# Attention on one core: score and value-sum matmuls alternate by pair of heads instead of by unit of four heads

## What is computed

```python
proj = quant4(x) @ ternary_weight(Wqkv_w).T + Wqkv_b      # q, k and v are views of it
q, k = (rotary(q, N), rotary(k, N))
ql, kl = (q @ U, k @ U)
att = jnp.einsum('bhnr,bhmr->bhnm', ql, kl) / math.sqrt(dk)
y = jax.nn.softmax(att, axis=-1) @ v
...
x = _layernorm(x + attention(x), axis=-1)
x = _layernorm(x + ffn(x), axis=-1)      # gated feed-forward, hidden width 1024, four layers
```

## Time and profile before

| | |
|---|---|
| Median of 3 runs | 2857.3 us (2856.99 to 2858.01) |
| Profiled execution: its own time | 2857.96 us |
| Profiled execution: span in the trace | 2856.3 us |
| Setup, until the first scores | 0 to 262 us |
| Attention | 262 to 2145 us |
| Feed-forward and end | 2145 to 2856 us |
| Busy over the span | PE 88%, ACT 74%, PE weight loads 37%, DVE 21%, POOL 11% |

### The profile page before, as it was taken

One profiled execution on the slowest core, in us unless ns is written; L12 is line 12 of the kernel. 1 busy time (PEld: TensorE's weight loads), 2 busy tenths in 40 slices (PEclk: granted clock), 3 DMA queues, 4 the chain that ended last, 5 costly groups with the idle time before them and its releaser, 6 DMA issues.

```text
span 2856.3 us, 40002 instructions
## 1 busy us (share of the span) xinstructions
PE 2508.4 (88%) x15895; PEld 1048.4 (37%) x15895; DVE 610.1 (21%) x1164; ACT 2124.8 (74%) x2360; POOL 311.4 (11%) x277
## 2 busy tenths in 40 slices
PE   2432999999999999999999999999995999999998
PEld 2220222222222222222222222222224888888887
DVE  7870000000000000000000000000005555655653
ACT  1222999999999999999999999999992223222232
POOL 2442888500000000000000000000000000000000
PEclk9765999999999999999999999999997999999999
DMA  1438444433333233323323333332222011001100
GB/s 60 130 119 228 103 99 104 93 64 63 64 63 67 58 63 63 71 64 63 62 58 67 64 64 63 69 66 60 59 45 48 1 23 22 22 0 22 22 8 16
DMA packets 94888, 178.42 MB, mean 62 GB/s; under 512 B 30432, under 2 KB 56064, under 8 KB 94208
## 3 DMA queue, kind: packets, MB, share of 16 engines
q1 hardware_dynamic: 90624, 153.05, 24.8%
q0 software_dynamic: 4096, 23.07, 3.0%
HBM read 150.63 MB, written 25.43 MB: 62 GB/s over the span
## 4 chain that ended last, share of the span: by engine, by line
ACT 34%; issue 32%; PE 25%; DVE 6%; DMA 2%; SPq 1%; ACTq 1%; DVEq 0%
ACT PB L270 34%; PE PS L517 16%; PE PS L502 4%; PE PS L529 2%; DVE TD L1060 1%; DMA KSL<-KSD 1%; ACTq L268 1%; PE PS L909 1%; DVE xq L1045 0%; DVE rq L1065 0%; DVE rq L1064 0%; DVE V L1048 0%; DVE khl L1068 0%; SPq L763 0%; DMA QSD<-shr 0%
## 5 line engine op out<-in xcount | busy, mean ns | idle before, releaser
L270 ACT ACTIVATE PB<-PS 128x1024 f32<-128x1024 f32 x2048 | 1877.7, 1237 | 1.4 <-PE PS L236 1.4
L245 PE MATMUL PS<-PB,V 128*17 128x512 f32 x8192 | 1079.3, 599 | 0.3 <-ACT PB L270 0.3
L236 PE MATMUL PS<-QSL,KSL 49*128 49x512 f32 x4096 | 753.6, 446 | 171.1 <-DMA KSL<-KSD 52.3
L236 PEld LDWEIGHTS PS<-QSL,KSL 49*128 49x128 f32 x4096 | 306.0, 185 | 1113.3 <-ACT PB L270 1060.9
L280 DVE STREAM_TRANSPOSE accS<-PS 128x512 f32<-128x512 f32 x32 | 22.9, 717 | 1874.5 <-PE PS L245 1874.5
L592 ACT ACTIVATE hfr<-PS,s 128x512 f32<-128x512 f32 x128 | 86.8, 689 | 300.5 <-PE PS L517 300.4
L245 PEld LDWEIGHTS PS<-PB,V 128*17 128x17 f32 x8192 | 136.0, 95 | 378.6 <-issue 364.1
L517 PE MATMUL PS<-hidden_ar,wh1r 128*128 128x512 f32 x1024 | 237.5, 391 | 0.0
L517 PE MATMUL PS<-hidden_br,wh2r 128*128 128x512 f32 x1024 | 235.3, 390 | 0.0
L517 PEld LDWEIGHTS PS<-hidden_br,wh2r 128*128 128x128 f32 x1024 | 191.7, 188 | 39.4
L517 PEld LDWEIGHTS PS<-hidden_ar,wh1r 128*128 128x128 f32 x1024 | 190.7, 188 | 40.1 <-DVE hfr L681 0.5
(11 more groups left out here) (135 smaller groups left out, 954.2 us busy)
## 6 DMA issues: line engine op xcount, KB each, us to landing
KSL<-KSD SPq DMA_DIRECT2D x256, 256.0 KB, 4.3
KSL<-KSD SPq DMA_DIRECT2D x256, 128.0 KB, 5.0
yq<-in_mlp POOLq DMA_DIRECT2D x44, 256.0 KB, 3.1
QSL<-QSD SPq DMA_DIRECT2D x64, 132.0 KB
QSD<-qhl SPq DMA_DIRECT2D x32, 256.0 KB
KSD<-khl SPq DMA_DIRECT2D x64, 128.0 KB
xg<-in_x SPq DMA_DIRECT2D x8, 512.0 KB, 5.7
QSL<-QSD SPq DMA_DIRECT2D x64, 64.0 KB
```

Of the source, the lines that this page charges most:

```text
L236: ins = pe.matmul(PS[:, 2 * (pair % SLOTS) + e, :], KSL[r, q % 2, s, k * P:(k + 1) * P], QSL[r, b % 2, s, :], start=True, stop=True, tile_ ...
L245: ins = pe.matmul(ACC[i * VW:i * VW + DK + 1, :], V17[:, HT * h + u, c, :], PB[:, (2 * unit + i // 2) % RING, (i % 2) * QW:(i % 2 + 1) * Q ...
L270: act.activation(PB[:, pair % RING, :], PS[:, slot:slot + 2, :].rearrange("p a b -> p (a b)"), ACT.Exp).then_inc(at["probs_ready"], 1)
```

## The change

`sums_pe` gets an argument `s` and issues two of the four heads of a unit: heads 0 and 1 with `s` = 0, heads 2 and 3 with `s` = 1. Only the second half increments `probs_free`, so ACT and DVE see it once for each unit as before. `attend_pe` now waits for one pair of exponentials, issues one pair of scores and then the value sums of that one pair, and does so twice for each unit. The wait for `acc_saved` stands before the first half's sums, and now behind one pair of scores where it was behind two. The number of matmuls, their operands and their shapes are the same.

```diff
-        def sums_pe(pe, at, unit, hb):
+        def sums_pe(pe, at, unit, hb, s):
+
             kt = unit % KT
             c, u = divmod(kt, HT)
-            for i in range(BL):
+            for i in (2 * s, 2 * s + 1):
                 h = hb * BL + i
                 ins = pe.matmul(ACC[i * VW:i * VW + DK + 1, :], V17[:, HT * h + u, c, :],
                                 PB[:, (2 * unit + i // 2) % RING, (i % 2) * QW:(i % 2 + 1) * QW],
                                 start=kt == 0, stop=kt == KT - 1, tile_position=(0, i * VW))
-            ins.then_inc(at["probs_free"], 1)
+            if s == 1:
+                ins.then_inc(at["probs_free"], 1)
...
             for unit in range(units):
-                pe.wait_ge(at["probs_ready"], n0 * PAIRS + (2 * unit + 2 + one))
-                for pair in (2 * unit + 3, 2 * unit + 4):
+                b = unit // KT
+                for k in range(2):
+                    pair = 2 * unit + SLOTS + k
+                    pe.wait_ge(at["probs_ready"], n0 * PAIRS + (2 * unit + 1 + k + one))
                     if pair < 2 * units:
                         scores_pe(pe, at, n0, pair)
-                b = unit // KT
-                if unit % KT == 0:
-                    pe.wait_ge(at["acc_saved"], n0 + (b + 1 + one))
-                sums_pe(pe, at, unit, b % NBLK)
+                    if unit % KT == 0 and k == 0:
+                        pe.wait_ge(at["acc_saved"], n0 + (b + 1 + one))
+                    sums_pe(pe, at, unit, b % NBLK, k)
```

## The result

| | before | changed |
|---|---|---|
| Median | 2857.3 us (2856.99 to 2858.01) | 3858.7 us (3858.24 to 3859.76, 4 runs) |
| Ratio, 95% interval | | 1.351 [1.348, 1.353] |
| Profiled execution, span | 2857.96, 2856.3 us | 3858.96, 3857.3 us |
| PE / ACT busy over the span | 88% / 74% | 94% / 61% |
| Attention, first scores to last sums | 262 to 2145 us | 261 to 3145 us |

The change makes the kernel 35% slower.

A forecast was written before the change was run, and what follows sets the result against it. PE replaces ACT as the bound: attention ends at 265.8 + 2048 x 1.40 + 15.2 + 3 - 1.3 = 3149.9 us, 1005 us later than before; added to 2857.96 us, this gives 3863 us, range 3640 to 3930 us.

The forecast's parts named there:

- ACT had set the pace and PE had 10% of slack: Attention before the change: ACT needs 1.83 us a unit, PE 1.64 us, leaving PE 0.19 us.
- A half-step of 0.43 + 0.44 + 0.53 = 1.40 us: Changed attention on PE: scores to first pass, first to second pass, second pass to scores; exceeds ACT's 0.917 us.
- A pass costs the same for two heads as for four: Value sums on PE: a two-head pass takes 0.44 us, as with four heads.
- The end of a block, 15.2 us: Wait for `acc_saved` before the next block's sums: 0.49 us more, 31 times.
- The start and the tail: Attention's ends: first two or three half-steps at clock 0.50 add 3 us; last three, without scores, save 1.3 us.
- Rival 1: PE's turn back to scores: weight loads hidden beside the last sums, half-step 1.30 us, kernel 3658 us; chance 10%.
- Rival 2: Sums' passes: two heads take 0.22 us; 2858 us with hidden weights (3%), about 2970 us with exposed ones (3%).
- rival 3: PE's turns between scores and sums: each costs more, half-step 1.44 to 1.55 us, kernel 3945 to 4170 us; chance 7%.
- Rival 4: PE in the attention: granted clock falls to 0.50, half-step about 2.55 us, kernel over 6000 us; chance 2%.
- What the profile would show: Attention's trace: ACT's share about 65%, record gap 0.16 us, PE's waits for ACT from 1023 to a handful, clock 1.00.

The follow-up runs named there:

- split waits: Kernel before, same groups of four scores and four sums, but a separate wait for each pair's exponentials; 2857.2 us, ratio 1.0003.
- small turns in every second unit: Kernel before plus a 16-column value matmul between the two pairs of scores, in every second unit only; 2863.3 us, ratio 1.0019.
- later small turns: Kernel before plus a 16-column value matmul between each unit's two pairs of scores, from the second block on; 3009.4 us, ratio 1.054.
- kernel with equal shapes: Changed kernel with one value matmul per pair over 64 rows, tile shape as the scores'; 5368 us, or 3263.6 us with 128 rows in the first block.
- kernel with small turns: Kernel before plus a 16-column value matmul between the two pairs of scores in every unit, from the first on; 4513 us, ratio 1.580.
- 256 columns in the small groups: Kernel before plus a one-head value matmul streaming 256 columns instead of 16 between each unit's two pairs of scores; 3416.5 us, ratio 1.195.

## Why the prediction was right

- **ACT had set the pace and PE had 10% of slack.** Right. The kernels with split waits and with small turns in every second unit stay within 0.2% of the kernel before. The later small turns add 0.35 us a unit to PE and (3009 - 2857) / 992 = 0.15 us to the kernel, so the slack took 0.20.
- **A half-step of 0.43 + 0.44 + 0.53 = 1.40 us.** Right as a sum, and its parts are now measured apart: two passes more cost 679 us (with what of them PE's slack took), and turns and weights 0.30 us a unit, as forecast. The sequence of one pair of scores and then sums at the attention's end gave the first term, and the one late unit the last; both views were a few rows out of thousands.
- **A pass costs the same for two heads as for four.** Right, to 0.015 us. The lone pass of 0.43 us had been the evidence.
- **The end of a block, 15.2 us.** Right: 14 us, with 0.46 us each where 0.49 were forecast.
- **The start and the tail.** Both were forecast a little too long. The first two half-steps took 2.55 and 2.49 us, 2.2 us more than two of 1.40, where the forecast had 3. From the last scores at 3142.81 to the end of the sums at 3145.5 it is 2.7 us, where the forecast's terms make 4 x 1.40 - 1.3 = 4.3. I had not seen that halves with nothing between them share passes. With 0.9 us less at the blocks' ends, and the attention beginning 1.1 us earlier in this execution, which is luck, they are the 4 us between forecast and result. Between the third half-step's scores at 269.56 and the last ones at 3142.81 lie 2042 half-steps; less 31 waits of 0.46 us that is 1.400 us each.
- **Rival 1, hidden weights (10%).** It did not come. The loads do run ahead in the kernel with equal shapes, so it is the change of shape that keeps them back, unless it is the rows in use, which the runs don't separate from it.
- **Rival 2, two heads for half the price (6%)**, and **rival 3, dearer turns (7%).** Excluded by the runs.
- **Rival 4, the clock (2%).** It did not come for the changed kernel, but my reason against it was wrong. I wrote that PE would be busier in time than where the clock was full. The kernel with small turns has PE busy in 3520.00 of 3520.00 us and was granted 0.50. In these runs busy time did not speak for the clock; the chance should have been larger.
- **What the profile would show.** ACT's busy share of the attention is 2080.20 / 2860 = 73%, not 65%. I had divided its pace, 0.917 us, by 1.40. But the record of one ACTIVATE went from 1.24 to 1.02 us once it no longer starts right behind another, so its share is 1.02 / 1.40, and the gap between records is 0.38, not 0.16 us. The rest of that list came as written, the 35 waits for ACT before scores being the handful.

## What to carry to other kernels

Matmuls that share the array in tiles are paid by the pass: splitting a group of four into two groups of two with other work between them doubles the passes and saves nothing, while adding matmuls to a pass with free quarters is almost free. Going from scores to sums or back cost 0.10 us here, and the exposed weights of 128 columns another 0.10, so gather as much as possible of one kind before turning. Giving both kinds the same tile shape took this cost away, but only in a kernel that leaves out half of the sum. Before regrouping, look for the places in the trace where the old order already shows the new sequence, such as the first late iteration and the tail: here they gave the new period to 1%.

## What the runs showed of the hardware

The granted clock depended on what went before and not only on what ran at the time. These are the stretches of the first microseconds of the attention (same columns as in the earlier trace rows), in the kernel with small turns from the first unit:

```profile
262.00:272.00 10.00, 7.34 (x30) 2.61 (x34) 0.00 (x0) 7.45 (x8) 0.00 (x0) 0.50 1.11 212
272.00:282.00 10.00, 10.00 (x46) 2.58 (x42) 0.00 (x0) 5.45 (x7) 7.79 (x8) 0.50 0.18 47
```

and in the one whose first block has none:

```profile
262.00:272.00 10.00, 8.86 (x52) 2.45 (x52) 0.00 (x0) 9.04 (x10) 3.70 (x4) 0.78 0.70 134
272.00:282.00 10.00, 9.41 (x70) 2.29 (x68) 0.00 (x0) 10.00 (x12) 8.05 (x9) 1.00 0.59 118
```

Both kernels enter the attention at 0.50. Without the small groups the clock is granted in full within ten microseconds, and then it stays at 2.4 GHz through 31 blocks that have them. With them from the start it stays at 1.2 GHz to the end of the attention, and 32 of 1024 units decide between 4513 and 3009 us. The kernels with equal tile shapes show the same: 5368 us when they begin so, 3264 us when the first block goes over 128 rows. The kernel with 256 columns in the small groups has them from the first unit on and was granted the full clock. All runs of each kernel agreed within 0.3%, so this is no accident of one execution. Why PE's full occupation is not enough in the one case is not settled here. A profile with PE at 100% and a low clock from the first unit on is a reason to try another first block.
